# A one-hot's index row and equality block in a PSUM bank of VectorE alone, and additions in fours, in a graph-layer kernel

## The reference, cut to what matters

```python
h = relu(layernorm(x))                          # 6250 nodes x 128
s, v = h[:, :32] @ W_up_s, h[:, 32:] @ W_up_v   # one table row per node
w0, w1, w2, w3 = split(silu(silu(edge_feats @ A1 + b1) @ A2 + b2) @ A3)
ss, vs = s[sender], v[sender]                   # the gather, 200000 rows
mji = [ss*y_s*w0, (vs.y_v)*w3, ss*y_v*w1, vs*y_s*w2]
message = segment_sum(mji, receiver) / 10
out = x + [message_s @ W_out_s, message_v @ W_out_v]
```

## Time and profile before

| | before |
|---|---|
| median of 3 launches | 2030.14 us (2027.99 to 2030.99) |
| profiled launch | 2042.36 us |
| its span, first to last instruction | 2040.6 us |
| mean granted clock of TensorE | 0.846 of 2.4 GHz |
| busy in the span: PE, POOL, DVE, ACT | 76%, 74%, 46%, 20% |
| chain that ended last: POOL's gathers, issue | 71%, 24% |

### The profile page before, as it was taken

One profiled execution on the slowest core, in us unless ns is written; L12 is line 12 of the kernel. 1 busy time (PEld: TensorE's weight loads), 2 busy tenths in 40 slices (PEclk: granted clock), 3 DMA queues, 4 the chain that ended last, 5 costly groups with the idle time before them and its releaser, 6 DMA issues.

```text
span 2040.6 us, 47831 instructions
## 1 busy us (share of the span) xinstructions
PE 1554.5 (76%) x16198; PEld 948.7 (46%) x16198; DVE 930.3 (46%) x2232; ACT 417.8 (20%) x836; POOL 1515.8 (74%) x1627
## 2 busy tenths in 40 slices
PE   5868777677777787776887768877787776877775
PEld 3444454444544445544545434444445444454444
DVE  4444444444444444444444444444444444444443
ACT  3212221111111111112122211221121111211211
POOL 4777777777777777777777777777777777777774
PEclk8897888988889878889778897888878889788987
DMA  8222222222222222222222222222222222222222
GB/s 225 57 59 57 58 57 59 56 59 57 59 57 58 57 58 56 59 56 58 56 59 58 58 58 56 59 56 59 56 59 56 58 57 58 57 58 57 59 56 100
DMA packets 110964, 128.22 MB, mean 63 GB/s; under 512 B 70498, under 2 KB 83074, under 8 KB 110820
## 3 DMA queue, kind: packets, MB, share of 16 engines
q0 software_dynamic: 50336, 102.64, 20.2%
q1 hardware_dynamic: 60420, 25.36, 4.8%
q10 hardware_dynamic: 192, 0.02, 0.0%
HBM read 121.46 MB, written 6.43 MB: 63 GB/s over the span
## 4 chain that ended last, share of the span: by engine, by line
POOL 71%; issue 24%; POOLq 1%; PE 0%; DMA 0%; DVE 0%; SPq 0%; ACT 0%; DVEq 0%
POOL rows L515 71%; POOLq L510 1%; POOLq L512 0%; POOLq L520 0%; PE pss L736 0%; DMA rows<-node_table,src_in 0%; PE psw L714 0%; DMA src_in<-in_src 0%; PE psx L755 0%; SPq L470 0%; DVE msgs L640 0%; PE psx L746 0%; DVE xT_sb L656 0%; DVEq L648 0%; ACT sums L556 0%
## 5 line engine op out<-in xcount | busy, mean ns | idle before, releaser
L515 POOL DMA_INDIRECT rows<-node_table,src_in x1563 | 1500.0, 960 | 488.7 <-issue 476.1
L736 PE MATMUL pss<-msgs,onehot 128*32 128x64 f32 (+1 forms) x12544 | 337.3, 255 | 445.9 <-DVE msgs L640 444.0
L638 DVE TENSOR_TENSOR msgs<-rows,psw 128x256 f32<-128x256 f32 x392 | 165.2, 421 | 1035.4 <-DMA rows<-node_table,src_in 1012.6
L736 PEld LDWEIGHTS pss<-msgs,onehot 128*32 128x32 f32 x12544 | 265.4, 120 | 697.7 <-DVE msgs L640 689.1
L714 PE MATMUL psw<-a_bd,h 128*128 128x256 f32 x1568 | 567.3, 496 | 3.6
L640 DVE TENSOR_TENSOR msgs<-rows,psw 128x768 f32<-128x768 f32 x392 | 371.2, 947 | 0.0
L714 PEld LDWEIGHTS psw<-a_bd,h 128*128 128x128 f32 x1568 | 328.2, 232 | 86.4 <-issue 26.0
L550 ACT ACTIVATE h<-ps,b_sb 128x512 f32<-128x512 f32 x196 | 134.7, 687 | 1045.4 <-PE ps L704 1045.4
L704 PE MATMUL ps<-h,a_bd 128*128 128x512 f32 x392 | 255.6, 741 | 0.9 <-ACT h L550 0.9
L698 PE MATMUL ps<-ef_in,a_bd 16*128 16x512 f32 x392 | 238.9, 691 | 15.3 <-DMA ef_in<-in_efT 13.7
L623 DVE TENSOR_TENSOR onehot<-eq,attr_in 128x1024 f32<-128x1024 f32 x196 | 238.8, 1218 | 0.0
(11 more groups left out here) (60 smaller groups left out, 137.3 us busy)
## 6 DMA issues: line engine op xcount, KB each, us to landing
rows<-node_table,src_in POOLq DMA_INDIRECT x1563
ef_in<-in_efT SPq DMA_DIRECT2D x98, 64.0 KB
xT_sb<-in_xT SPq DMA_DIRECT2D x7, 448.0 KB, 8.4
x_sb<-in_x SPq DMA_DIRECT2D x7, 448.0 KB, 8.0
attr_in<-in_attr SPq DMA_DIRECT2D x98, 32.0 KB
out_T<-xT_sb SPq DMA_DIRECT2D x1, 3136.0 KB, 8.9
node_table<-tab_sb SPq DMA_DIRECT2D x7, 256.0 KB, 3.9
src_in<-in_src SPq DMA_DIRECT2D x98, 8.0 KB
```

What stands on the lines that cost most here:

```text
L515: pool.indirect_dma_start(out=rows[:, QT * p + t, :], out_offset=None, in_=table, in_offset=bass.IndirectOffsetOnAxis(ap=src_in[:, b, at:a ...
L638: dve.tensor_tensor(m[:, :, :, 0, :], g[:, :, 0, :].unsqueeze(2).broadcast_to([P, QT, 2, MUL]), w[:, :, :, 0, :], ALU.mult)
L736: last = nc.tensor.matmul(to, onehot[:, o, QT * half + w, c, :], moving, start=(half == 0 and c == 0), stop=(half == 1 and c == 3), skip_g ...
```

## The change

`iota_f` and `eq` leave SBUF for the second bank of `psx`: `iota_ps` takes its first 32 columns, `eq` the next 256. Only VectorE touches that bank in the round. `pso` moves to the first bank, behind `pst`. Since a bank now holds both what TensorE turns and what VectorE adds from, the wait for the additions of the oct before moves from `project` to `turn`. `WINDOW_LAG` becomes 8, and the four additions of an oct are made together at the start of every even quad, ahead of its messages. In `scale` and `equal` the first input then comes from PSUM and the second from SBUF; no instruction is added to or removed from the round. The conversion of the index row moves from VectorE's start to behind its last table rows.

```diff
-WINDOW_LAG = OW + 2
+WINDOW_LAG = 2 * OW
...
-        pso = psx[:, 1, 0:OW * W]
+        pso = psx[:, 0, CH:CH + OW * W]
+        iota_ps = psx[:, 1, 0:W]
+        eq = psx[:, 1, W:W + HT * W].rearrange("p (t w) -> p t w", w=W)
...
-                dve.wait_ge(iota_built, 3)
-                dve.tensor_copy(iota_f[:, :], iota_i[:, :]).then_inc(rounds_step, 1)
...
+                def place_iota():
+                    dve.wait_ge(iota_built, 3)
+                    dve.wait_ge(up_done, 2 * NCH)
+                    dve.tensor_copy(iota_ps, iota_i[:, :]).then_inc(rounds_step, 1)
...
+                place_iota()
                 count_rounds()
...
-                        dve.tensor_tensor(eq[:, :, :], iota_f[:, :].unsqueeze(1).broadcast_to([P, HT, W]),
+                        dve.tensor_tensor(eq, iota_ps.unsqueeze(1).broadcast_to([P, HT, W]),
...
-                            eq[:, :, :].unsqueeze(2).broadcast_to([P, HT, 4, W]),
+                            eq.unsqueeze(2).broadcast_to([P, HT, 4, W]),
...
-                            late = not (first and n < 0)
+                            if p % 2 == 0 and not (first and n < 0):
+                                for i in range(OW):
+                                    add_window(j, n + i)
                             messages(j, p, quad_tiles(p) if last else QT)
                             if ahead and p % 2 == 0:
                                 relative(*ahead)
-                            if late:
-                                add_window(j, n)
-                            if ahead:
-                                (equal, scale)[p % 2](*ahead)
-                            if late:
-                                add_window(j, n + 1)
+                                equal(*ahead)
+                            elif ahead:
+                                scale(*ahead)
...
                     def turn(j, o):
                         pe.wait_ge(sums_copied, j * OCTS + o + 1 + SUMS_CREDIT)
+                        pe.wait_ge(window_added, j * 2 * QB + OW * o + ADD_CREDIT)
                         pe.wait_ge(turned_copied, j * OCTS + o + TURN_CREDIT)
...
                     def project(j, o):
                         pe.wait_ge(turned_copied, j * OCTS + o + 1 + TURN_CREDIT)
-                        pe.wait_ge(window_added, j * 2 * QB + OW * o + ADD_CREDIT)
```

More of the change, by code:

```diff
@@ L114, in gnn_layer_kernel @@
         iota_i = sb("iota_i", [P, W], I32)
-        iota_f = sb("iota_f", [P, W])
         start_row = sb("start_row", [1, NW])
@@ L140, in gnn_layer_kernel @@
         onehot = sb("onehot", [P, HOT_SLOTS, HT, 4, W])
-        eq = sb("eq", [P, HT, W])
         rel = sb("rel", [P, HT])
```

## The result

| | before | after |
|---|---|---|
| median, measured side by side | 2029.41 us (2027.99 to 2030.99) | 2015.84 us (2015.58 to 2016.20) |
| ratio | | 0.9937 (95% interval 0.9924 to 0.9949) |
| profiled launch | 2042.36 us, span 2040.6 | 2015.58 us, span 2013.8 |

The change made the kernel 13.6 us faster by the medians, 0.63%. Between the two profiled launches it is 26.8 us.

A forecast was written before the change was run, and what follows sets the result against it. GpSimd's chain of 1563 gathers and gaps was taken as the bound. Profiled, 2042.36 less 24.5 of stalls plus 0.6 of tail gave 2018.5 us; for the 2030.14 median a gain of 21 gave 2009 us, range 2002 to 2021.

The forecast's parts named there:

- the branch of 2003 to 2014: Whole launch: the main forecast, about 2009 us from a gain of 21 on the unprofiled median; chance 0.60.
- rival C: Gathers in unprofiled launches: they stall half as much, leaving 11.7 us to gain, so 2018.5 us; chance 0.27.
- The bound and the sum: GpSimd's gathers and gaps bound the round; 2042.36 less 24.5 excess plus 0.6 gives 2018.5 us profiled, a span of 2016.7.
- From the profiled launch to the median: Launches without a profile, 12.2 us lower at 2030.14: gain between 11.7 and 23.9, taken as 21, giving 2009 us.
- The rule for a stall: A gather starting under scale: excess is end of scale minus start of gather, less 0.12 us; 24.5 us over 196 scales.
- rival A: Scale's second input: the lock hangs on an input's place, so stalls stay; 2011 to 2047 us; chance 0.06.
- Form of the inputs: Scale and equal with PSUM first, SBUF second: one SBUF input each, so the gathers' 24.5 us excess goes.
- Rival B: Gathers' stall: it is not scale's, so nothing goes and the tail adds 0.6, 2030.7 us; chance 0.04.
- D: VectorE's relative takes scale's place in a shifted phase, losing 16 us of the gain, 2025 us; chance 0.03.
- Duration of scale from PSUM: Scale on VectorE: 1210 ns with a PSUM input against 1218 before, so nothing gained.
- Additions in fours, and the turn: Even quads: four additions take 1.60 us under 2.65 of cover; they end 0.3 before the turn needs them; GpSimd unaffected.
- Tail: After the last gather: the last turn now waits for the four additions, adding 0.6 us with the signal.

The follow-up runs named there:

- the second launch: The kernel before, unchanged, traced in another launch: 2040.85 us against 2041.78, ratio 0.9997; the profiled launch took 2039.72.
- the half-microsecond delay: The kernel before with a VectorE reduction of 384 numbers ahead of each scale: 2119.68 us against 2033.59, ratio 1.0425.
- the two doses: The kernel before with a VectorE reduction ahead of each scale, of 384 or of 980 numbers: 2119.68 and 2022.21 us against 2033.59.

## Why the prediction was right, and where it wasn't

It gave 2009 us in a range of 2002 to 2021; 2015.84 was measured, in the direction forecast. The time lies not in the branch of 2003 to 2014 that had most of the chance, but near the time of rival C, which the range took in. Step by step:

- **The bound and the sum.** Right. The excess of 24.5 us by the earlier trace rows was the whole gain on the chain; the gathers' sum fell by 25.1 and their mean to the median. The sum for the profiled launch gave a span of 2016.7; 2013.8 was measured, and of the 2.9 between them 2.0 are the earlier first gather.
- **From the profiled launch to the median.** This step was mis-sized. The 12.2 us between them were put mostly on the profile (gain of 21, "because the steady pair repeats the mean and so the phase is the loop's own"). The phase is not the loop's own: with one order on VectorE it is 0.120 to 0.162 us in three groups of runs, and beside the kernel after the kernel before had 13.6 us to lose. The case with 11.7 of gain (C, 2018.5) was the near one in size, but not by its cause: the second launch shows that profiling costs nothing here. So it is in part luck that the range held.
- **The rule for a stall.** Its size was right: end of scale less start of the gather less 0.12, by the earlier trace rows and again under the half-microsecond delay. Its reading, that the gather needs something "0.12 us into its work", was wrong. Scales that start 0.07 and 0.09 behind a gather's start don't hold it, so the need comes at the start. The 0.12 then belongs to the end of scale; that it is the time behind its last reading fits, but no run here shows it. The wrong reading made rival A's cliff come too early (for a scale that ends under 0.10 behind a start, where the edge is a scale that starts 0.04 ahead of one), and with it the upper end of the expectation for the additions in fours.
- **Form of the inputs.** Right, and rival A has fallen: with PSUM first and SBUF second, a scale that lay 0.58 over a gather cost it nothing. Rival B has fallen to the two doses. D has fallen too, though not by the earlier trace rows: that relative starts 0.05 behind its gather, so it could not hold it. Relative takes 0.16 us; one that starts 0.04 ahead of a gather has 0.12 of it left at the start, less than the 0.126, so by the rule it costs nothing in any phase. No trace shows a gather held by it.
- **Duration of scale from PSUM.** 1210 ns were worked out, 1217 measured, 1218 before. Equal went from 425 to 432:

```profile
L628 DVE TENSOR_TENSOR onehot<-psx,attr_in 128x1024 f32<-128x1024 f32 x196 | 238.5, 1217 | 0.0
L619 DVE TENSOR_TENSOR psx<-psx,rel 128x256 f32<-128x256 f32 x196 | 84.8, 432 | 6.8
```

- **Additions in fours, and the turn.** The cover on GpSimd's side held; the one ahead of the turn was smaller than worked out. The groups of the waits in the kernel after, and last the turn's in the kernel before:

```profile
DVE msgs L643 <- DMA rows<-node_table,src_in: 779.6, 385, 3.6
...
DVE xT_sb L661 <- DVE xT_sb L661: 159.9, 367, 0.5
PEld psx L751 <- DVE xT_sb L661: 92.5, 120, 0.8
PEld psx L751 <- issue: 70.0, 75, 1.5
...
PEld psx L746 <- issue: 160.2, 195, 1.5
```

VectorE's wait for gathers fell from 1012.6 us to 779.6. Within the round later additions stand 0.64 apart (0.19 and 0.45 idle), not the 0.47 of the tail's, and four took 1.78 and not 1.60. So the 0.3 us ahead of the turn were used up in 120 cases, in which an addition is what comes last before it. It cost next to nothing: the loading of weights pauses ahead of the turns for 92.5 + 70.0 = 162.5 us in all, and did for 160.2 before the change. As predicted, it did not reach GpSimd.

- **What the change's order did.** The prediction priced the earlier start of scale (0.10) only under rival A. It is the piece that was left out: with all tiles in SBUF the order took 11.0 us off by itself, and an earlier scale without the new order 12.8 in another group. That made no difference to the sum, since PSUM takes what the order leaves and no stall can be taken away twice. But it says which part does the work: with the scales where they stand in the kernel after, two SBUF inputs would have cost 5.6 us by the rule (an estimate; that kernel was not run there), so the phase alone would have taken most of the 25.1 between the two profiled launches, as PSUM alone takes all of it whatever the phase.
- **Tail.** 0.6 us predicted, 0.3 measured. The last turn does wait for an addition now, as said:

```profile
1999.89 0.19 DVE L661 TENSOR_TENSOR xT_sb<-xT_sb,psx 128x32 f32 x1 [0.28 <-DVE xT_sb L661]
...
2000.18 0.41 PE L751 MATMUL psx<-identity,sums 128*128 128x128 f32 x2 [1.14 <-ACT sums L561]
```

The copy of the sums had ended at 1999.49 (1999.11 and 0.38 long), so the releaser that the row names had long been done, and the addition that ended at 2000.08 is what the turn waited for.

## What to carry to other kernels

Where GpSimd's DMAs are the bound, compare the mean and the median of that one line: here an excess that nothing on its queue explained was another engine's, and the row that overlaps its start named it. Give a long VectorE operation that runs beside them at most one SBUF input, as scale has here. If no PSUM bank is to be had, shift it against the gathers first; that cost nothing and gave half of the gain or more here, but a scale just beyond the edge costs 1.04 us each time, and half a microsecond the wrong way cost 86 in all. A gain that is made of stalls by phase differs from one group of runs to another, so its size is to be forecast as a range over phases and not from one profiled launch.

## What the runs showed that was not expected

- More work on an idle engine made the kernel faster: 980 numbers reduced ahead of each scale, 228.6 us of added VectorE time, 2022.2 us against 2033.6. The prediction had no such case; the expectation ahead of that run did.
- The kernel before has three speeds in three groups of runs (2029.4, 2033.6, 2041.8 us), the kernel after one in two of them (2015.8, 2015.6). The speed goes with the time of the gathers' packets; that the packets set it, through the phase, was not tried by itself.
- Gathers have a median of 947 ns in two kernels of one group, those with the equality block in PSUM, and of 944 in the two others of it. The cause is open; it is worth some 3.3 us.
